# Query maxima of an attention tower: tiles of every seventh query, and rows filled by 28-byte transfers

## The reference

```python
q = jnp.einsum('btd,hrd->bhtr', x, Q)
k = jnp.einsum('bud,hrd->bhur', x, K)
scores = jnp.einsum('bhtr,bhur->bhtu', q, k) / sqrt(d)
attn = jax.nn.softmax(scores, axis=-1)
ctx = jnp.einsum('bhtu,bud->bhtd', attn, x)
out = jnp.einsum('bhtd,hde->bte', ctx, VO)
```

## Time and profile before

| what | value |
|---|---|
| median of 3 runs | 662.3 us (660.54 to 670.1) |
| the profiled execution | 657.45 us |
| its span | 655.6 us |
| busy in the span: PE, DVE, ACT, POOL | 589.2, 401.8, 338.0, 70.4 us |
| the attention passes | about 187 to 584 us of the span |

### The profile page before, as it was taken

The page is one execution under the profiler, slowest core; times in us unless marked ns, Lnnn a source line. Parts: engine busy times, 40 slices in busy tenths (PEclk is TensorE's granted clock), DMA queues, the critical chain, the costliest instruction groups (busy, mean ns, idle before and its releaser), DMA issues.

```text
span 655.6 us, 10594 instructions
## 1 busy us (share of the span) xinstructions
PE 589.2 (90%) x3080; PEld 332.6 (51%) x3080; DVE 401.8 (61%) x996; ACT 338.0 (52%) x710; POOL 70.4 (11%) x80
## 2 busy tenths in 40 slices
PE   0695988998999999999999999999999999997993
PEld 0451444553445565565665665665565565452441
DVE  3846475125687767766766766775775777245661
ACT  0466775664645545544644554554554555545511
POOL 0000000000893000000000000000000000012000
PEclk9998899998999999999999999999999999997998
DMA  7500000000632222322322322322322320000014
GB/s 159 212 0 1 0 1 0 1 0 13 154 97 73 73 68 73 77 58 74 82 54 71 89 54 70 90 54 69 85 61 60 84 70 18 2 1 0 1 43 105
DMA packets 21987, 37.65 MB, mean 57 GB/s; under 512 B 5561, under 2 KB 15225, under 8 KB 21705
## 3 DMA queue, kind: packets, MB, share of 16 engines
q1 hardware_dynamic: 21816, 37.12, 22.1%
q10 hardware_dynamic: 144, 0.20, 0.2%
HBM read 6.07 MB, written 2.41 MB: 13 GB/s over the span
## 4 chain that ended last, share of the span: by engine, by line
PE 79%; DVE 7%; ACT 4%; issue 3%; DMA 3%; POOL 2%; SPq 1%; ACTq 0%; DVEq 0%; POOLq 0%
PE P L681 76%; DMA X<-x 2%; DVE mx L1379 2%; POOL acc L667 2%; PE P L697 2%; ACT PT L585 1%; ACT L482 1%; DVE part L1420 1%; DVE xhat L1205 1%; ACT g L622 1%; DVE xs L1274 1%; PE P L1080 0%; SPq L371 0%; PE P L937 0%; DVE gate_s L1262 0%
## 5 line engine op out<-in xcount | busy, mean ns | idle before, releaser
L585 ACT ACTIVATE PT<-P 112x392 f32<-112x392 f32 x448 | 188.5, 497 | 167.7 <-PE P L681 166.6
L1379 DVE TENSOR_REDUCE mx<-P 112x1 f32<-112x392 f32 x448 | 232.8, 558 | 54.9 <-PE P L681 53.4
L681 PE MATMUL P<-PT,XVs 112*64 112x392 f32 x896 | 175.5, 507 | 0.0
L681 PE MATMUL P<-Ks,Qs 96*112 96x392 f32 x448 | 164.8, 372 | 2.5 <-DVE mx L1379 1.8
L681 PE MATMUL P<-Qs,Ks 98*112 98x392 f32 x448 | 153.6, 348 | 9.0 <-ACT PT L585 9.0
L681 PEld LDWEIGHTS P<-Ks,Qs 96*112 96x112 f32 x448 | 77.4, 175 | 91.9 <-issue 60.9
L681 PEld LDWEIGHTS P<-Qs,Ks 98*112 98x112 f32 x448 | 78.3, 176 | 19.3 <-ACT PT L585 14.1
L681 PEld LDWEIGHTS P<-PT,XVs 112*64 112x64 f32 x896 | 53.0, 136 | 61.8 <-issue 43.1
L1406 DVE RECIPROCAL zi<-P 98x1 f32<-98x1 f32 x32 | 5.4, 169 | 75.9 <-PE P L681 75.9
L681 PE MATMUL P<-VBs,CT 128*98 128x130 f32 (+1 forms) x320 | 37.2, 263 | 0.6 <-ACT CT L593 0.6
L681 PEld LDWEIGHTS P<-VBs,CT 128*98 128x98 f32 x320 | 36.4, 165 | 2.3 <-ACT CT L593 1.3
(11 more groups left out here) (183 smaller groups left out, 545.5 us busy)
## 6 DMA issues: line engine op xcount, KB each, us to landing
Qs<-QKH SPq DMA_DIRECT2D x64, 98.0 KB, 2.2
Ks<-QKH SPq DMA_DIRECT2D x64, 98.0 KB, 2.1
XVs<-XV SPq DMA_DIRECT2D x32, 196.0 KB, 2.5
Qs<-QKL SPq DMA_DIRECT2D x32, 98.0 KB, 2.1
Ks<-QKL SPq DMA_DIRECT2D x32, 98.0 KB, 2.1
X<-x SPq DMA_DIRECT2D x4, 588.0 KB
out<-OT SPq DMA_DIRECT2D x24, 98.0 KB
wa<-table_a SPq DMA_DIRECT2D x1, 2207.5 KB, 8.5
```

What stands on the lines that cost most here:

```text
L585: nc.scalar.activation(PT[:, u % PTS, c * HALF:(c + 1) * HALF], P[0:T, SCORE_BANK + half_in_loop(s, u, c) % RING, 0:HALF], ACT.Exp, scale= ...
L681: return nc.tensor.matmul(dst, lhsT, rhs, start=start, stop=stop, **more)
L1379: nc.vector.tensor_reduce(mx[:, s % 2, c, t:t + 1], bank(n)[0:T, :], AX.X, ALU.max)\
```

## The change

- A max tile u no longer takes queries 112u to 112u+111, but queries 7t+u for t from 0 to 111: the weights are every seventh element of a row of `Qs`, 28 bytes apart.
- So partition t of `mhl` holds the negative maxima of queries 7t to 7t+6, side by side. `rows_to_stack` sends `mhl` itself: two transfers of 112 pieces, 28 bytes each, that stand one behind the other in the row.
- The turn on TensorE, the copy on VectorE, the tile `mT`, and both semaphores `turn_full` and `turn_done` with all waits on them are gone.
- VectorE may overwrite `mhl` only after the rows of the head before have landed, so the second instruction of `minus_max` now waits for `mrow_in` of that head.

The diff, less its blank lines, declarations and removed calls:

```diff
             def rows_to_stack(i, s):
-                sync.wait_ge(turn_done, 4 * i + s + 1)
+                sync.wait_ge(mhl_ready, 4 * i + s + 1)
                 for r in range(2):
-                    sync.dma_start(Qs[96 + r:97 + r, s, :].bitcast(F32), mT[r * NT:(r + 1) * NT, :].bitcast(F32)).then_inc(mrow_in[s], 16)
+                    sync.dma_start(Qs[96 + r:97 + r, s, :].bitcast(F32), mhl[:, r * NT:(r + 1) * NT].bitcast(F32)).then_inc(mrow_in[s], 16)
...
-                if b >= 2:
-                    pe.wait_ge(turn_done, 1)
...
-                mm(P[0:T, bank_, 0:HALF], Qs[0:96, s, t * T:(t + 1) * T], Ks[0:96, s, c * HALF:(c + 1) * HALF]).then_inc(max_full, 1)
-            def max_turn(i, s):
-                pe.wait_ge(mhl_ready, 4 * i + s + 1)
-                nc.tensor.transpose(P[0:2 * NT, 7, 0:T], mhl[:, :].bitcast(F32), Bt("ident", T)[:, 0:T]).then_inc(turn_full, 1)
+                mm(P[0:T, bank_, 0:HALF], Qs[0:96, s, :].rearrange("p (t u) -> p u t", u=NT)[:, t, :], Ks[0:96, s, c * HALF:(c + 1) * HALF]).then_inc(max_full, 1)
...
-                if not (isinstance(n, int) and n > NH - 3):
-                    pe.wait_ge(turn_done, n + 3)
...
-                        if q == 1 and not (final and s == 3):
-                            if not (first and s < 2):
-                                pe.wait_ge(proj_done, 4 * i + s - 1)
-                            max_turn(i + (s == 3), (s + 1) % 4)
...
-                if j == 8:
-                    pe.wait_ge(xv_done, 2)
-                    max_turn(0, 0)
...
                 elif part_ == 1:
                     own()
+                    if not (isinstance(i, int) and i + s == 0):
+                        vector.wait_ge(mrow_in[(s - 1) % 4], 32 * (i + (s > 0)))
                     nc.vector.tensor_scalar(mhl[:, 0:NT], mxf[:, :], -1.0, None, ALU.mult).then_inc(vec_step, steps.one())
...
-            def max_rows(i, s):
-                vector.wait_ge(turn_full, 4 * i + s + 1)
-                nc.vector.tensor_copy(mT[:, :], P[0:2 * NT, 7, 0:T]).then_inc(turn_done, 1)
```

More of the change, by code:

```diff
@@ L123, in build @@
         mhl = sb(ctx, "mhl", [T, 2 * NT], F32R)
-        mT = sb(ctx, "mT", [2 * NT, T], F32R)
         reg1 = ExitStack()
@@ L255, in build @@
         max_full, max_done, mhl_ready = sem("max_full"), sem("max_done"), sem("mhl_ready")
-        turn_full, turn_done = sem("turn_full"), sem("turn_done")
         st_full, exp_done, av_done, ctx_done = sem("st_full"), sem("exp_done"), sem("av_done"), sem("ctx_done")
@@ L1445, in four_heads @@
                             minus_max(*following, 1)
-                        if u == 3 and not (final and s == 3):
-                            max_rows(*following)
                         if u == 5 and s < B - 1 and final:
@@ L1454, in _ @@
                         minus_max(0, 0, part_)
-                if j == 8:
-                    max_rows(0, 0)
                 for c in range(2):
```

## The result

The changed kernel is slower: 677.33 us median (675.33 to 683.73), against 663.44 us for the kernel before (660.54 to 670.1); ratio 1.026, 95% interval 1.022 to 1.030. The profiled execution took 683.73 us, its span is 681.9 us.

The account below looks back on a forecast made before the run. TensorE's issue was taken to bound each pass. The turn's 3.1 us plus the copy's 0.2 us gave 3.3 us less, from 662.3 to 659.0 us, with a range of 652 to 672 us.

Parts of the forecast that it names:

- the price of the stepped weights: Max-half weight loads with elements 28 bytes apart: record stays at 175 ns, no time added.
- the 28 ns: Extra time per max load, over 120 bare loads, beyond which the change loses its 3.3 us gain.
- The turn: Turn leaves TensorE between batch 1's last score half and context product: 0.10 us a head, 3.1 us in all.
- The copy: VectorE's copy to `mT` goes: worth nothing inside the passes, 0.2 us ahead of them.
- SyncE's order: Row transfers on SyncE issue earlier and land at 391.05, wanted at 397.25: hidden, cost 0.
- VectorE's wait: VectorE's new wait for the previous head's rows before overwriting `mhl`: over before it is reached, cost 0.
- the `turn_done` waits: Waits before the output product and before two turned value tiles: removing them is worth 0.
- Rival B: Stepped load slower, at most doubled; bare loads at batch starts add up to 10.8 us, 669.8 us; chance 0.24.
- Inside a batch it can double for nothing: Max loads inside a batch need 0.08 to 0.09 us and are allowed up to 0.18 us, one matmul.
- Rival C: Load slower by 143 ns or more: 17.2 us bare plus 15.9 us inside batches, 692.1 us; chance 0.10.
- Rival D: The 224 pieces a head land too late; first score half waits some 14 us, 450 us in all; chance 0.03.
- E: The gap from score half to context product stays at 0.37 us: 662 us, no change; chance 0.07.

Follow-up runs that it names:

- the straight pieces alone: Changed kernel with the max weights of before (112 queries side by side), keeping the straight 28-byte transfers and no turn: 658.31 us median, ratio 0.992.
- score-first kernel: Changed kernel with the score half issued before the max half in each pair: 684.71 us median, ratio 1.031 to the kernel before.
- run in pairs: Changed kernel with max tiles in pairs, weights 8 bytes apart, rows sent in 8 transfers a head: 660.42 us median, ratio 1.000 to the kernel before.

## Why the prediction was wrong

The step that failed is the price of the stepped weights: "I take no change". Measured, the record is 282 ns, +107, well past the 28 ns that the forecast named as the sign of its being wrong. The argument for it was that the nearest row to such a load is the load itself. It is near in everything but the one thing that the change alters, so it said nothing about that; and the thought that a load has time to spare, at half a stream's pace, holds up to a step of two elements (8 bytes) and not up to seven.

The prediction's own sum for a longer load does better than its choice. With 107 ns, 120 bare loads cost 12.8 us, and 300 others 0.017 us each over the 0.18 that are covered, 5.1 us: 662.3 - 3.3 + 17.9 = 676.9 us, where 677.3 were measured. That it comes so close is partly luck. It leaves out the three held loads of each pass, about 0.05 us more each and 4.5 us in all, and on the other side the shorter wait in the passes that begin a group (7 x 0.3 us).

- *The turn*, 0.10 us: right, by the straight pieces alone (12.13 to 12.03 us) and by the step of 0.27 us in the changed kernel. So was the reason for not taking its record of 0.26 us.
- *The copy, SyncE's order, VectorE's wait, the `turn_done` waits*: nothing each, as forecast. Landing takes 2.0 us where I took 2.2, and the two issues are quicker, not slower.
- *Rival B*, a load up to doubled, had the mechanism and a chance of 0.24. Its price of 0.36 us a pass (four bare loads at 0.09) was half of the measured 0.74. The bare starts were right, 4 x 0.10. "Inside a batch it can double for nothing" holds where the load is covered: at 230 ns it costs nothing there, and the 282 ns are just past doubled (0.107 for 0.09) and cost 0.02 to 0.03 us. It is wrong for three max halves in a pass whose load is held by the ring. The rows for that were in the trace before: the fourth load of each batch starts 0.08 to 0.09 us ahead of its matmul (385.87 for 385.95), and in some passes the second of the first batch does (385.14 for 385.22). I read that as the lead that is needed and not as a load with nothing to spare.
- *Rival C's* upper bound, +143 ns, was on the right side, and its sum of 33 us was too high. The result, 677.3 us, lies between B and C, 5 us over the top of the range.
- *The rule of the Trainium skill* (SBUF — State Buffer, section Door 1: The DMA port swizzle) against the change was the better guide than the row, and the record of 282 ns agrees with it. I gave it no number, since it has none.
- *Rival D*, late pieces: out, at 2.0 us. *E*, the gap that stays: out, by the step of 0.27 us.

## What to carry to other kernels

Before the weights of a matmul get a stride, ask how many bytes of each 16-byte line are used: with two fp32 elements a line the load kept its pace to 5 ns, with one it took 0.10 us more for 112 columns. No run here gives a stride to the moving operand. What a longer load costs is counted at the places where nothing covers it: at batch starts, and wherever its own wait for a buffer holds it back. A layout change often has a half that pays; time both halves apart, and look for the tile shape in which both can be had.

## What was not expected of the hardware

- Transfers in pieces of 28, 8 and 4 bytes between partitions landed 1.9 to 2.0 us after their issue, where the `Qs<-QKH` transfers of 98 KB took 2.1; for the 448-byte pieces no view gives a landing. An issue of 112 pieces took SyncE 0.6 us, one of 7 pieces 0.75 us (the median of `Qs<-mT` before). What costs is the number of issues: 8 took 5.0 to 5.8 us.
- One wait of 1.32 us on TensorE in a pass, between stretches in which it is busy, was followed by up to 6.8 us at half clock each time in the score-first kernel; in the kernel before, a wait of 1.05 us at the same place was not, nor was any of the 0.7 to 1.1 us in the other runs. Without the wait the clock held. The length of a wait does not decide alone: behind the passes TensorE waits 2.52 us for ScalarE in several kernels, and the clock fell behind it in the kernel before (at 594.7 us) and did not in the run in pairs.
